# Expert routing by scattered rows, and twelve expert tiles placed around the last sequence

## What is computed

```python
def reference(x, wq, wk, wv, wo, wg1, wg2, norm_w, centroids, ln_g, ln_b, w1, b1, w2, b2):
    x = x + attention(_layernorm(x), wq, wk, wv, wo, wg1, wg2, norm_w)
    return x + ffn(_layernorm(x), centroids, ln_g, ln_b, w1, b1, w2, b2)

def ffn(input_features, centroids, ln_g, ln_b, w1, b1, w2, b2):
    x = input_features.reshape(-1, 256)
    aff = x @ centroids.T                          # (4096, 8)
    assign = jnp.argmax(aff, axis=1)
    order = jnp.argsort(assign)
    xs, es = x[order], assign[order]
    alpha = jax.nn.sigmoid(jnp.take_along_axis(aff[order], es[:, None], axis=1))
    y = jnp.zeros_like(xs)
    for e in range(8):
        h = _layernorm(xs, ln_g[e], ln_b[e])
        h = jax.nn.relu(h @ w1[e].T + b1[e])       # 1024 hidden units
        y = y + jnp.where((es == e)[:, None], xs + h @ w2[e].T + b2[e], 0.0)
    return (alpha * y + (1.0 - alpha) * xs)[jnp.argsort(order)]
```

## Time and profile before

| | us |
|---|---|
| median of 3 runs | 679.5 (677.5 to 682.62) |
| the profiled execution, its own time | 674.16 |
| its span, first to last instruction | 672.3 |
| TensorE busy | 593.8 (88%) |
| VectorE busy | 343.8 (51%) |
| ScalarE busy | 280.1 (42%) |
| GpSimd busy | 226.1 (34%) |

### The profile page before, as it was taken

How to read it: one execution, slowest core, us unless ns; L and a number is a source line. 1 busy time by engine, 2 the same in 40 slices (tenths; PEclk the granted TensorE clock), 3 DMA queues, 4 the chain that set the end, 5 groups by cost and what they waited for, 6 DMA issues and landing times.

```text
span 672.3 us, 12520 instructions
## 1 busy us (share of the span) xinstructions
PE 593.8 (88%) x3638; PEld 501.2 (75%) x3639; DVE 343.8 (51%) x864; ACT 280.1 (42%) x671; POOL 226.1 (34%) x384
## 2 busy tenths in 40 slices
PE   3979999999999999977632799999999999999992
PEld 2547676777768677766421799999999999999992
DVE  2395968879595959677147123322322332332331
ACT  3554667575676767552430232223223223223220
POOL 6614262515334351611122122233233233233221
PEclk9999999999999999979665799999999999999997
DMA  9900014141302212020222964455455455455300
GB/s 325 402 12 1 0 33 95 32 94 33 83 12 75 53 32 64 33 63 33 63 63 86 347 232 179 175 217 205 172 203 218 168 202 218 179 189 225 119 29 2
DMA packets 26844, 83.48 MB, mean 124 GB/s; under 512 B 3437, under 2 KB 13039, under 8 KB 20656
## 3 DMA queue, kind: packets, MB, share of 16 engines
q1 hardware_dynamic: 21120, 67.98, 30.4%
q0 software_dynamic: 4992, 14.45, 5.8%
q10 hardware_dynamic: 688, 0.52, 0.2%
HBM read 70.33 MB, written 13.52 MB: 125 GB/s over the span
## 4 chain that ended last, share of the span: by engine, by line
PE 71%; DVE 9%; issue 4%; ACT 2%; POOL 1%; DMA 1%; DVEq 0%; ACTq 0%; POOLq 0%
PE bank_a L1133 21%; PE bank_c L1147 20%; PE bank_l L889 5%; PE bank_a L901 4%; PE bank_c L1003 4%; PE bank_a L930 3%; DVE arena L1198 2%; DVE arena L1209 2%; PE bank_b L981 2%; PE bank_a L946 2%; PE bank_a L939 2%; PE bank_b L980 1%; PE bank_b L1121 1%; PE bank_b L967 1%; PE bank_c L1020 1%
## 5 line engine op out<-in xcount | busy, mean ns | idle before, releaser
L1463 DVE TENSOR_TENSOR arena<-bank_a,b_col 128x512 f32<-128x512 f32 x78 | 54.0, 692 | 189.5 <-PE bank_a L1133 175.7
L1133 PEld LDWEIGHTS bank_a<-masks,arena 128*128 128x128 f32 x1248 | 147.0, 194 | 1.9
L1133 PE MATMUL bank_a<-masks,arena 128*128 128x128 f32 x1248 | 147.1, 277 | 0.0
L1147 PE MATMUL bank_c<-w_sb,arena 128*128 x624 | 141.5, 380 | 1.4 <-ACT arena L864 0.9
L1147 PEld LDWEIGHTS bank_c<-w_sb,arena 128*128 128x128 f32 x624 | 115.5, 190 | 16.4 <-issue 2.3
L889 PEld LDWEIGHTS bank_l<-arena,k_mix 128*128 128x128 f32 x448 | 65.2, 197 | 47.2 <-ACT k_mix L685 34.6
L1198 DVE TENSOR_TENSOR arena<-arena 128x256 f32<-128x256 f32 x224 | 89.6, 442 | 9.3 <-PE bank_l L889 9.3
L864 ACT ACTIVATE arena<-arena 128x512 f32<-128x512 f32 x78 | 45.0, 622 | 107.4 <-PE bank_c L1147 102.9
L889 PE MATMUL bank_l<-arena,k_mix 128*128 128x128 f32 x448 | 72.9, 288 | 14.2 <-DVE arena L1209 12.2
L854 ACT ACTIVATE masks<-bank_b,b_col,g_col 128x128 f32<-128x128 f32 x78 | 31.4, 453 | 129.1 <-PE bank_b L1121 129.1
L901 PE MATMUL bank_a<-arena 128*128 128x512 f32 x160 | 81.9, 611 | 0.0
(11 more groups left out here) (137 smaller groups left out, 747.8 us busy)
## 6 DMA issues: line engine op xcount, KB each, us to landing
arena<-w SPq DMA_DIRECT2D x39, 1024.0 KB
routed_rows<-arena SPq DMA_DIRECT2D x8, 1026.0 KB, 7.8
arena<-x SPq DMA_DIRECT2D x16, 512.0 KB, 5.6
w_sb<-w SPq DMA_DIRECT2D x8, 1024.0 KB, 14.0
arena<-b SPq DMA_DIRECT2D x1, 1024.0 KB, 4.8
arena<-routed_rows,take_now POOLq DMA_INDIRECT x39, 4.1
out<-k_mix,put_now POOLq DMA_INDIRECT x39, 2.5
arena<-wk SPq DMA_DIRECT2D x1, 256.0 KB, 3.9
```

The lines of the kernel that those rows point to most:

```text
L1133: m = pe.matmul(bank_a[k // 4][:, k % 4 * P:(k % 4 + 1) * P], w1_now[t.par][:, i * F + k * P:i * F + (k + 1) * P], xl_t[t.par % 2][:, i * ...
L1147: m = pe.matmul(bank_c[p][:, 0:D], h_act[:, k * P:(k + 1) * P], w2_sb[:, bass.ds(e * (FC * D) + k * D, D)], start=(k == 0), stop=(k == FC ...
L1463: dve.tensor_tensor(h_sb[:, n * 512:(n + 1) * 512].rearrange("p (k t) -> p k t", t=P), bank_a[n][:, :].rearrange("p (k t) -> p k t", t=P), ...
```

## The change

- **Rows by expert.** `routed_rows` becomes `rows_by_expert`: one region of 4096 rows for each expert, 514 numbers a row (the token's own number is the last). After sequence c's affinities, `route(c)` on VectorE (six small instructions) makes its one-hots and running counts, `ranks(c)` on TensorE (two matmuls, a third for two of the sequences) and `slots(c)` on VectorE (two instructions) give each token's row, one step later. GpSimd's `scatter_rows(c)` then scatters the sequence with four indirect DMAs, in place of SyncE's L495. It stands ahead of the decay tree.
- **Tile tables in two parts.** After five sequences (EARLY = 5) there are at least 12 full tiles; `early_tables` (22 VectorE instructions in step 7) lists them. `last_tables`, in three parts between turns 4 to 6, lists the other 27. The inversion by one-hot matrices is gone.
- **Order.** Step 9 is gone. Tiles 0 to 3 have their w1 and rows fetched in step 8, and the last sequence's norm, transposes, `out_proj`, residual, affinities and rows are written out by hand between tiles 0 to 3.
- **GpSimd's turn** is now scatter(n) and then gather(n+4), unrolled for all tiles; the index copies for the gather go, and the scatter's index is the gathered token number plus `skip`.
- **x is fetched two steps ahead**, by SyncE at the start of a step.
- `down` writes `bank_l` instead of `bank_c`; buffers are laid out so that the first tiles' fit over what is dead in step 8.

The core of the diff:

```diff
-    rows = nc.dram_tensor("routed_rows", (N, RW), F32, kind="Internal").ap()
+    rows = nc.dram_tensor("rows_by_expert", (E * REGION, RW), I32, kind="Internal").ap()
...
-            for i in range(NSEQ + 2):
+            for i in range(NSEQ + 1):
...
-                if nxt is not None and b is not None:
-                    need_apart(sp, s_xn, TJ, b, TJ)
-                    sp.dma_start(tiles(x_sb[nxt.par]), seq_rows(x_t, nxt)).then_inc(s_x[nxt.par], 16)
+                ahead = before(nxt, -1) if nxt is not None else None
+                if ahead is not None and number(ahead) < NSEQ:
+                    need_apart(sp, s_xn, TJ, a, TJ)
+                    sp.dma_start(tiles(x_sb[ahead.par]), seq_rows(x_t, ahead)).then_inc(s_x[ahead.par], 16)
                 if b is not None:
                     need_apart(sp, s_x1, 2, b, 0)
                     sp.dma_start(tiles(x_res), seq_rows(x_t, b)).then_inc(s_xres, 16)
-                if c is not None:
-                    need_apart(sp, s_zn, TJ, c, TJ)
-                    need_apart(sp, s_base, TJ, c, TJ)
-                    need_apart(sp, s_alpha, 1, c, 1)
-                    sp.dma_start(seq_rows(rows_t, c), tiles(row_sb, RW)).then_inc(s_row_out, 16)
-            pipeline(sp, step)
-            need(sp, s_y, 2, Step(NSEQ // 2 - 1, 1, 2), 2)
-            sp.wait_ge(s_row_out, 16 * NSEQ + 16)
-            sp.dma_start(b2_sb, b2.rearrange("e f -> (e f)").partition_broadcast(P)).then_inc(s_b2, 16)
-            def turn(t):
+                if a is None:
+                    need(sp, s_o, 2, c, 2)
+                    need(sp, s_og, 2, c, 2)
+                    need(sp, s_state, 5, c, 5)
+                    need(sp, s_dz, H, b, H)
+                    need(sp, s_q0, 1, b, 1)
+                    for n in range(SLOTS):
+                        fetch_w1(tile(n))
...
+            def scatter_rows(c):
+                n = number(c)
+                need(pool, s_slot, 2, c, 2)
+                pool.tensor_copy(slot_i[:, n * TJ:(n + 1) * TJ], slot_f[:, n * TJ:(n + 1) * TJ]).then_inc(s_sloti, 1)
+                need_apart(pool, s_sloti, 1, c, 1)
+                need_apart(pool, s_zn, TJ, c, TJ)
+                need_apart(pool, s_base, TJ, c, TJ)
+                need_apart(pool, s_alpha, 1, c, 1)
+                for j in range(TJ):
+                    t = n * TJ + j
+                    pool.indirect_dma_start(out=rows, out_offset=bass.IndirectOffsetOnAxis(ap=slot_i[:, t:t + 1], axis=0),
+                                            in_=tiles(row_sb, RW)[:, j].bitcast(I32), in_offset=None).then_inc(s_row_out[n >= EARLY], 16)
...
+                if c is not None and number(c) > 0:
+                    scatter_rows(before(c, 1))
+                if a is None:
+                    pool.wait_ge(s_idx, 2)
+                    need(pool, s_o, 2, c, 2)
+                    need(pool, s_state, 5, c, 5)
+                    pool.wait_ge(s_row_out[0], 16 * TJ * EARLY)
+                    for n in range(SLOTS):
+                        gather(n)
...
+            def gather(n):
+                p = n % SLOTS
+                need(pool, s_yo, 1, Step(n // SLOTS - 1, p, SLOTS), 1)
+                pool.indirect_dma_start(out=gathered[p].bitcast(I32), out_offset=None, in_=rows,
+                                        in_offset=bass.IndirectOffsetOnAxis(ap=take_idx[:, n:n + 1], axis=0)).then_inc(s_rows[p], 16)
+            def scatter(n):
+                p = n % SLOTS
+                pool.wait_ge(s_rows[p], 16 * (n // SLOTS) + 16)
+                pool.tensor_scalar(put_of[:, n:n + 1], gathered[p][:, 2 * D + 1:2 * D + 2], skip[:, n:n + 1], None, ALU.add).then_inc(s_put, 1)
+                pool.wait_ge(s_put, n + 1)
+                need(pool, s_yo, 1, Step(n // SLOTS, p, SLOTS), 1)
+                pool.indirect_dma_start(out=out, out_offset=bass.IndirectOffsetOnAxis(ap=put_of[:, n:n + 1], axis=0),
+                                        in_=y_out[p], in_offset=None, bounds_check=N - 1, oob_is_err=False).then_inc(s_out[p], 16)
+            def turn(n):
+                scatter(n)
+                if n + SLOTS < TILES:
+                    gather(n + SLOTS)
...
+            scatter_rows(LAST_BUT_ONE)
+            double_norm(LAST_SEQ)
+            for n in range(3):
+                turn(n)
...
+            scatter_rows(LAST_SEQ)
+            for n in range(3, NA - SLOTS):
+                turn(n)
...
+            gains(tile(0))
+            gains(tile(1))
+            for j in range(TJ):
+                o_norm(LAST_SEQ, j)
+            relu(tile(0))
+            for i in range(DC):
+                o_copy(LAST_SEQ, i)
+            gains(tile(2))
+            turn(tile(1))
+            relu(tile(2))
+            x1_copies(LAST_SEQ)
+            gains(tile(4))
+            rows_of(LAST_SEQ)
+            turn(tile(3))
+            alphas(LAST_SEQ)
...
+            def ranks(c):
+                need(pe, s_route, 6, c, 6)
+                need(pe, s_x1t, DC, c, DC)
+                if number(c) in (EARLY - 1, NSEQ - 1):
+                    pe.matmul(bank_c[1][:, E * TJ:E * (TJ + 1)], ones[:, :], upto5[:, :, TJ], start=True, stop=True).then_inc(s_total, 1)
+                pe.matmul(bank_c[1][:, 0:E * TJ], earlier, hot5[:, :, 1:TJ + 1], start=True, stop=False)
+                pe.matmul(bank_c[1][:, 0:E * TJ], ones[:, :], upto5[:, :, 0:TJ], start=False, stop=True).then_inc(s_rank, 1)
...
+            need(pe, s_og, 2, c, 2)
+            z_transposes(tile(0))
+            z_transposes(tile(1))
+            ranks(LAST_BUT_ONE)
+            need(pe, s_at0, H, c, H)
+            up(tile(0))
+            o_transposes(c, 0)
+            o_transposes(c, 1)
+            pe.wait_ge(s_w2, 16 * E)
+            need(pe, s_pick, 2 * LEVELS, c, 2 * LEVELS)
+            turn(tile(0))
+            for half in range(2):
+                for j in range(2):
+                    out_proj(c, half, j)
+            turn(tile(1))
+            x1_transposes(c)
+            turn(tile(2))
+            for n in range(DC * TJ):
+                affinity(c, n)
+            turn(tile(3))
+            ranks(c)
+            for n in range(4, NA):
+                turn(tile(n))
...
+            def early_tables():
+                tile_counts(region_e, 0)
+                tile_experts(0, NA)
+                tile_rows(region_e, NA)
+                dve.tensor_scalar(take_idx[:, 0:NA], column_of(4, NA), row_at[:, 1:2], None, ALU.add).then_inc(s_idx, 1)
...
+            def slots(c):
+                n = number(c)
+                need(dve, s_rank, 1, c, 1)
+                if n in (EARLY - 1, NSEQ - 1):
+                    dve.wait_ge(s_total, 1 + (n == NSEQ - 1))
+                    own(dve.tensor_copy(end_e, bank_c[1][:, E * TJ:E * (TJ + 1)]))
+                dve.tensor_tensor(by_e(place), bank_c[1][:, 0:E * TJ].rearrange("p (e j) -> p j e", e=E),
+                                  hot5[:, :, 1:TJ + 1].rearrange("p e j -> p j e"), ALU.mult).then_inc(s_slot, 1)
+                need(dve, s_slot, 2, c, 1)
+                dve.tensor_reduce(slot_f[:, n * TJ:(n + 1) * TJ], by_e(place), AX_X, ALU.add).then_inc(s_slot, 1)
...
+                if c is not None and number(c) > 0:
+                    slots(before(c, 1))
...
+                if nxt is None:
+                    early_tables()
                 if b is not None and c is None:
                     centre()
                 output(b, c, a)
+                of(c, route)
...
+            slots(LAST_BUT_ONE)
             for n in range(2):
-                bias_h(Step(0, 0, SLOTS), n)
+                bias_h(tile(0), n)
+            turn(tile(0))
+            for half in range(2):
+                residual(c, half)
+                need(dve, s_x1, 2, c, half + 1)
+                sums("u", x1, (2 * half, 2 * half + 1))
+            moments("u", c)
+            dve.wait_ge(s_b2, 16)
+            turn(tile(1))
+            turn(tile(2))
+            affinities(c)
+            route(c)
+            turn(tile(3))
+            slots(c)
+            for part in range(3):
+                turn(tile(4 + part))
+                last_tables(part)
+            for n in range(7, NA):
+                turn(tile(n))
```

427 lines of the change are left out of this document (201 added, 226 removed).

## The result

The kernel after the change takes **651.1 us** (median of 4 runs, 650.17 to 655.08), the kernel before 679.1 us on the same chip (677.5 to 682.62, 4 runs). The ratio is 0.9592, 95% interval 0.9537 to 0.9647: 28 us faster. The profiled execution took 650.17 us, its span 648.4.

The account below looks back on a forecast made before the run. VectorE and TensorE take turns limiting the steps; TensorE bounds the tiles, after a hole from 337 to 375.2. 674.2 - 52.1 + 7.9 + 6.3 + 4.1 + 2.2 - 1.7 = 640.9, plus 5.3 to the median: 646 us, range 633 to 662.

Parts of the forecast that it names:

- The first `up`: Tile 0's start after step 8: near 323.0 instead of 375.06, gain 52.1 us; near 329 with the steps' 6.3 us.
- VectorE in the steps: Attention steps: `route` and `slots` add 1.0 us a full step, 6.3 us in all; `early_tables` cost nothing.
- The last sequence's TensorE work: Between the first tiles: `out_proj`, transposes, affinities and `ranks` now stand there, costing 7.9 us.
- gather(7): Tile 7's rows, behind the last sequence's scatters on GpSimd: one TensorE stall of 4.1 us.
- The gather behind the scatter in each tile: GpSimd's turn in each tile: scatter first makes the path 0.17 us too long, 2.2 us over 27 tiles.
- the gather paces the tiles: Rival, tiles: gather data wait for the scatter's landing, 22 us in place of 2.2, taken as 660 us; chance 0.13.
- The clock: First `up` matmuls: right behind the outputs they run at full clock, giving back 1.7 us.
- everything hides: Rival: scatters have no gaps and VectorE's additions fall into waits, so steps, gather(7) and tiles cost nothing, 634 us; chance 0.17.
- GpSimd's late tree: Steps: scatters make the decay tree 2.2 us late, taken as 0; rival of longer steps, 13 us, 659 us, chance 0.09.
- The overlap happens: Start of tiles; its rival: w1 of tile 0 or first gathers late, half the hole stays, 672 us, chance 0.04.
- slower than before: Rival, tile loop: long landings under w1 loads push the path past 9.3 us and eat the gain; chance 0.02.

Follow-up runs that it names:

- doubled `route`: Changed kernel with six more small VectorE instructions behind `route` in each of the eight sequences: 659.81 us, ratio 0.9733 to the kernel before.
- gather first: Changed kernel with GpSimd issuing gather(n+4) ahead of the scatter of tile n: 647.1 us, ratio 0.9569 to the kernel before.
- both: Changed kernel with the gather ahead of the scatter and the last sequence's row scatters after turn 3: 642.9 us, 645.2 us when run again.
- less w1: Changed kernel fetching only a sixteenth of each w1 from tile 12 on, products using old weights: 649.0 us, ratio 0.9597 to the kernel before.

## Why the prediction was right, and where it was not

The forecast was 646 us, the result 651.1, inside 633 to 662. The sum itself, against the profiled execution, was 640.9 and came to 650.17, 9.3 us off; the 5.3 us that I added for the distance to the median (1 us this time) hid half of that. Term by term, for the profiled execution:

**The first `up`: right.** Forecast 329.3, found 329.53. From the last diagonal to it I had 36.9 us, and 0.8 for VectorE; it is 38.0. Inside it, the outputs end 34.5 us after the diagonal, where I had 34.3, and from there to the `up` are 3.4 us in place of 2.6: I had `route` there and left out the transposes of tiles 0 and 1 with ScalarE's copy between them. Ahead of that diagonal the sum is right for other reasons than mine:

**VectorE in the steps: too high a price a step, right sum by accident.** I took 1.0 us a step; it is 0.27 in each of steps 4 to 6 (37.28 against 37.01). The first seven sequences were to add 5.5 us up to the last diagonal; it is 5.4 us later, but with other parts. The route instructions run at the pitch I read the earlier trace rows, but the cover is 1.2 us, not the 0.7 us of waits that I counted. The 5.4 us are 1.8 at the start of the run (the clock of the first projections in this execution), 0.4 in steps 1 and 2, 1.6 in step 3, 0.8 in steps 4 to 6 and 0.8 in step 7, the one with `early_tables`, which I had hidden in full. The doubled `route` shows that the argument, VectorE paces, holds beyond the cover.

**The last sequence's TensorE work: right.** Beside the 7.25 us of a tile, turns 0 to 2 take 10.70, 8.14 and 9.29 us from one `down` to the next, 6.4 in excess, and `o_transposes` 0.87 and the `ranks` 0.6: 7.9, as forecast.

**gather(7): right place, 6.7 us in place of 4.1.** GpSimd's timeline of the change, and TensorE's at the same place:

```profile
373.33 1.02 POOL L609 DMA_INDIRECT rows_by_expert<-arena  x1 [1.09 <-issue]
...
377.20 0.97 POOL L609 DMA_INDIRECT rows_by_expert<-arena  x1 [0.30 <-issue]
378.21 0.31 POOL L667 TENSOR_SCALAR put_of<-arena,skip 128x1 int32<-128x1 f32 x1
379.34 1.04 POOL L670 DMA_INDIRECT out<-k_mix,put_of  x1 [0.82 <-POOL put_of L667]
380.68 0.99 POOL L661 DMA_INDIRECT arena<-rows_by_expert,take_idx  x1 [0.30 <-issue]
```

```profile
378.49 3.73 PE L1160 MATMUL bank_a<-masks,arena 128*128 128x128 f32 x32
386.74 0.69 PE L1148 MATMUL bank_b<-ident,arena 128*128 128x128 f32 x2 [4.52 <-DMA arena<-rows_by_expert,take_idx]
387.58 4.98 PE L1176 MATMUL bank_l<-w_sb,arena 128*128 x16 [0.16 <-issue]
```

TensorE wants the rows at 382.06, and I had 382.1. Indirect DMAs follow each other after 0.30 us, not 0.79, so the gather starts 1.4 us earlier than I had it (380.68 against 382.1). But it lands after 6.0 us, not 4.1. And behind an idle time of 4.5 us the next `down` falls to the lower level, 4.98 us in place of 3.46; this stall cost TensorE its clock besides, which my sum left out. Moving the rows behind turn 3 took this stall away, but left almost 3 of the 6.7 us at the tiles beside it.

**The gather behind the scatter in each tile: path right, its size wrong, 2.2 forecast and 5.7 found.** One miss in the change's timeline:

```profile
417.61 0.49 DVE L1562 SCALAR_TENSOR_TENSOR k_mix<-masks,arena 128x256 f32<-128x256 f32 x1
...
418.98 1.04 POOL L670 DMA_INDIRECT out<-k_mix,put_of  x1 [4.57 <-DVE k_mix L1562]
420.32 1.00 POOL L661 DMA_INDIRECT arena<-rows_by_expert,take_idx  x1 [0.30 <-issue]
...
425.56 0.44 PE L1148 MATMUL bank_b<-ident,arena 128*128 128x128 f32 x2 [0.45 <-DMA arena<-rows_by_expert,take_idx]
...
426.41 1.77 PE L1176 MATMUL bank_l<-w_sb,arena 128*128 x7 [0.41 <-issue]
```

0.88 + 1.04 + 0.30 + 5.2 to landing is 7.4 us, where 6.63 is allowed. With the median landing, 3.7, it would be 5.9 and no loss; I took one landing for all tiles and averaged, where 6 of the tiles behind gather(7) miss and each miss costs 0.6 to 1.5 us (TensorE's restart of 0.4 to 0.6 ahead of the `down` and 0.26 in the next tile among it). The rival "the gather paces the tiles" had the same path with the scatter's landing in it; that part is excluded by the landing times above, and its price of 14 us did not come.

**The clock: wrong.** I said that `up(0)` right behind the outputs would run at full clock and give back 1.7 us. It stands behind two waits, 0.78 us for VectorE's gating and 1.11 us for ScalarE's copy of tile 0, and takes 4.96 us: 1.4 lost. The term that failed: I had `up(0)` follow the outputs without an idle time. With these two waits open it was slow in eight of ten profiled executions and at full clock in two; with them covered it was at full clock in both. So the waits are the likely cause, and not a shown one. I read the Trainium skill ("TensorE: Matmul & The Clock Gate", Part 1) as saying that activity brings the clock back. The runs agree: behind the slow first `up` it is 1.00 from 337 to 375, with TensorE busy throughout.

**The end: a term that was missing.** From the start of the last scatter to the end of the span is 9.05 us before (663.25 to 672.3) and 11.75 after (636.65 to 648.4), 2.7 more, and 11.7 to 11.8 in the profiles of *gather first*, *both* and *less w1* too. The last scatters of the kernel after land in 2.1 to 2.2 us, so their landing is not it; what fills the rest no view shows, and I did not try it.

Together: 2.6 (gather(7)), 2.4 (the tiles: 5.7, less the 2.2 forecast and the 1.1 that the kernel before loses the same way), 1.4 (clock) and 2.7 (end) make 9.1 of the 9.3 us.

**The rivals.** Not everything hides: steps, gather(7) and tiles all cost. GpSimd's late tree does not lengthen the steps by making anyone wait for its results: the four scatters and the copy end at 127.3 in step 3 and the tree follows at once, as late as I had it, and no row shows a wait for it. But step 3 is 1.3 us longer than the steps behind it, and that goes with the moment at which the tree starts (last section): a cost for which I had taken 0, far from the rival's 13 us. The overlap happens, TensorE is full from 337 to 375. The loop never nears the 9.3 us from which it would have been slower than before: its longest path in the trace of the change is the 7.4 us above.

## What to carry to other kernels

When a change closes a hole of TensorE, look at the waits that are left on its edge: behind 0.8 and 1.1 us of idle time the first expert matmuls lost 1.1 to 2.0 us of clock in eight of ten executions, and none in the two in which eight small products in a free bank covered the waits. An effect read from one profiled execution has to be looked for in the others as well: two more had it without the cover. Put what the next tile waits for ahead of what nobody waits for on GpSimd's queue, and judge a DMA path by its longest landings, not by the median. Read cover by adding work until it costs (the doubled `route`), not from the waits alone; and of an offset that nothing in the profile explains, forecast none.
